# More table-sum steps in high and low parts, and VectorE constants read by pointer, in the product-key stage of an audio tower

## The reference

```python
k = einsum('bnhk,bnhkd->bnhd', kv_scores, keys_table[ind])
v = einsum('bnhk,bnhkd->bnhd', kv_scores, values_table[ind])
attn = softmax(where(causal, einsum('bihd,bjhd->bhij', q, k), neg))
out = einsum('bhij,bjhd->bhid', attn, v)
```

## Time and profile before

| what | value |
|---|---|
| median of 3 runs | 2059.56 us (2059.18 to 2062.91) |
| the profiled execution, its own time | 2059.58 us |
| its span | 2057.8 us, so 1.8 us lie around it |
| granted TensorE clock, mean | 0.97; 1.00 in every stretch of 200 us from 500 us on |
| busy, share of the span | PE 94%, PEld 73%, DVE 84%, ACT 72%, POOL 61% |
| third stage | from about 275 us to the end |

### The profile page before, as it was taken

How to read it: one execution, slowest core, us unless ns; L and a number is a source line. 1 busy time by engine, 2 the same in 40 slices (tenths; PEclk the granted TensorE clock), 3 DMA queues, 4 the chain that set the end, 5 groups by cost and what they waited for, 6 DMA issues and landing times.

```text
span 2057.8 us, 43660 instructions
## 1 busy us (share of the span) xinstructions
PE 1942.7 (94%) x11396; PEld 1509.4 (73%) x11396; DVE 1724.5 (84%) x5163; ACT 1486.5 (72%) x3091; POOL 1265.2 (61%) x1300
## 2 busy tenths in 40 slices
PE   5996649999999999999999999999999999999997
PEld 3983437777777777777777777777777777777776
DVE  3562659999989989999999899999999899999996
ACT  3564236787777777777777777787778777777775
POOL 2440106667766666677677667666766666676664
PEclk9998768999999999999999999999999999999998
DMA  3000030000100020001000100001000100010001
GB/s 97 1 0 0 1 103 16 18 14 19 62 20 19 19 62 18 18 17 59 18 19 19 58 23 19 19 19 60 17 17 16 60 19 19 19 61 19 19 17 27
DMA packets 118154, 58.06 MB, mean 28 GB/s; under 512 B 109712, under 2 KB 116048, under 8 KB 116813
## 3 DMA queue, kind: packets, MB, share of 16 engines
q1 hardware_dynamic: 115298, 56.75, 10.2%
q10 hardware_dynamic: 2795, 0.70, 0.2%
HBM read 24.55 MB, written 0.70 MB: 12 GB/s over the span
## 4 chain that ended last, share of the span: by engine, by line
PE 79%; issue 2%; DVE 1%; SPq 1%; DMA 1%; POOL 1%; ACT 1%; DVEq 0%; ACTq 0%; POOLq 0%
PE ps L988 27%; PE ps L996 15%; PE ps L979 15%; PE ps L1000 7%; PE ps L1038 4%; PE ps L1056 3%; PE ps L973 2%; PE ps L1048 2%; PE ps L1023 2%; SPq L931 1%; DMA k_X<-k_spl 1%; PE ps L1010 1%; PE ps L1016 1%; POOL k_W_low L1322 0%; PE ps L1039 0%
## 5 line engine op out<-in xcount | busy, mean ns | idle before, releaser
L1322 POOL TENSOR_TENSOR k_W_low<-k_W,k_W_high 128x688 fp32r<-128x688 f32 x513 | 852.3, 1661 | 379.0 <-ACT k_W_high L1164 379.0
L1159 ACT ACTIVATE k_W<-ps 128x688 f32<-128x688 f32 x1029 | 765.6, 744 | 391.3 <-PE ps L979 373.9
L1441 DVE SCALAR_TENSOR_TENSOR k_W<-ps,k_W 128x688 f32<-128x688 f32 x1028 | 888.8, 865 | 164.0 <-ACT k_W L1159 144.4
L988 PE MATMUL ps<-k_W,k_tab 128*128 128x344 f32 x2048 | 676.9, 453 | 0.0
L979 PE MATMUL ps<-k_X,k_sel 128*128 128x344 f16 x2058 | 473.8, 312 | 26.7 <-DMA k_X<-k_spl 13.5
L988 PEld LDWEIGHTS ps<-k_W,k_tab 128*128 128x128 f32 x2048 | 367.2, 190 | 127.2 <-issue 0.6
L1164 ACT ACTIVATE k_W_high<-k_W 128x688 fp32r<-128x688 f32 x513 | 395.4, 771 | 0.0
L996 PE MATMUL ps<-k_W_high,k_tab_high 128*128 128x344 f32 x1024 | 385.7, 379 | 0.0
L979 PEld LDWEIGHTS ps<-k_X,k_sel 128*128 128x128 f16 x2058 | 170.9, 99 | 216.0 <-issue 82.6
L996 PE MATMUL ps<-k_W_high,k_tab_low 128*128 128x344 f32 x1024 | 324.9, 320 | 0.0
L1000 PE MATMUL ps<-k_W_low,k_tab_high 128*128 128x344 f32 x1024 | 244.4, 320 | 0.0
(11 more groups left out here) (228 smaller groups left out, 2567.3 us busy)
## 6 DMA issues: line engine op xcount, KB each, us to landing
k_tab<-in_tables SPq DMA_DIRECT2D x9, 2048.0 KB, 7.2
k_X<-k_spl SPq DMA_TRANSPOSE x390, 2.4
k_xs<-x2T SPq DMA_DIRECT2D x33, 172.0 KB, 2.1
k_qT<-k_qs SPq DMA_DIRECT2D x33, 86.0 KB, 2.0
cst<-in_consts SPq DMA_DIRECT2D x1, 1024.0 KB, 19.0
wts<-in_weights SPq DMA_DIRECT2D x1, 896.0 KB, 13.0
cst<-in_consts SPq DMA_DIRECT2D x1, 874.5 KB, 16.7
xr<-in_xrows SPq DMA_DIRECT2D x1, 750.0 KB
```

Source lines behind the costliest of these rows:

```text
L988: mm = mm_(sums, tab[:, slot, at + k, :], W[:, d % RING, k, :], start=(d == 0 and k == 0), stop=(d == NDC - 1 and k == 1))
L1159: A(W[:, d % RING, :, :], ps[:, 2 * (d % 2):2 * (d % 2) + 2, 0:LOUT], ACT.Exp).then_inc(e_done, 1)
L1322: G.tensor_tensor(W_low[:, q % SPLIT_RING, :, :], W[:, d % RING, :, :], W_high[:, q % SPLIT_RING, :, :].bitcast(F32), ALU.subtract).then_i ...
L1441: V.scalar_tensor_tensor(W[:, d % RING, :, :], ps[:, 2 * (d % 2):2 * (d % 2) + 2, 0:LOUT], 0.0, W[:, d % RING, :, :], ALU.is_ge, ALU.mult) ...
```

## The change

Steps 1, 2, 3, 5, 7, 9, 10, 11, 13 and 15 are split: steps 2 and 10 join the eight. Of each window of 8 table chunks 6 are now held in parts (3 of 4 steps; tab_high and tab_low grow from 32 to 48 chunks a side, and an eighth of the table from two chunks to three). Ten steps are no multiple of the ring's 4, so `part_slot` also counts by the item's parity. P and PT of the attention now lie in parts of the constants' tile that are free by then. The attention output moves on PE from behind step 13 to behind step 14, and DVE's `add_output` from step 14 to step 15. The constants of `clamp_scores` and `floors` lie in a tile `bounds` of 128x4, filled once by four memsets at the start, and the four operations read them as 128x1 operands. Left out below: the handing of `cst` into the function, and the further argument `par` of `weights_high` and `weights_low` where they are called.

```diff
@@ -778,18 +778,18 @@
         NDC = NCH // 2
         WINDOW = (0, 2, 3, 1)
         STEPS = 6 + 6 + 6 + 1 + 3 + 3 + 2 + 3
-        SPLIT = (1, 3)
-        SPLITS = [d for d in range(NDC) if d % 4 in SPLIT]
+        SPLIT = (1, 2, 3)
+        SPLITS = [1, 2, 3, 5, 7, 9, 10, 11, 13, 15]
         NSPLIT = len(SPLITS)
-        NPART = 2 * NSPLIT // 8
-        FIRST_ROW = (2, 6)
+        NPART = len(SPLIT)
+        FIRST_ROW = (2, 5)
         RING, SPLIT_RING = 8, 4
         LEAD = 5
         MID0, MID1 = 6, 7
 
         tab = sb("tab", [128, 2, NCH, 128])
-        tab_high = sb("tab_high", [128, 2, 2 * NSPLIT, 128], F32R)
-        tab_low = sb("tab_low", [128, 2, 2 * NSPLIT, 128], F32R)
+        tab_high = sb("tab_high", [128, 2, 8 * NPART, 128], F32R)
+        tab_low = sb("tab_low", [128, 2, 8 * NPART, 128], F32R)
         wqh = sb("wqh", [128, 2, 128])
         wos = sb("wos", [128, H, D])
         pkw_sb = sb("pkw_sb", [DKEY, H, 128])
@@ -809,6 +809,8 @@
         small = sb("small", [128, 5, NT])
         MX, AM, FLOOR, DT, EDT = range(5)
         off = sb("off", [128, NT])
+        bounds = sb("bounds", [128, 4])
+        UPPER, LOWER, MARGIN, DEPTH = (bounds[:, k:k + 1] for k in range(4))
         ecs = sb("ecs", [128, NT, NCAND])
         zs = sb("zs", [128, NT])
         gain = sb("gain", [128, 2, NT])
@@ -826,11 +828,11 @@
         vw = sb("vw", [128, NT, D])
         qT = sb("qT", [128, 2, LOUT])
         qs = sb("qs", [64, LOUT])
-        P = sb("P", [128, NT, LOUT])
+        P = cst[:, CONST["cos"][0]:CONST["decay"][1]].rearrange("p (t s) -> p t s", t=NT)
         nmax = sb("nmax", [128, NT])
         zz = sb("zz", [128, NT])
         rz = sb("rz", [128, NT])
-        PT = sb("PT", [128, NT, LOUT])
+        PT = cst[:, CONST["sel"][0]:CONST["sel"][0] + NT * LOUT].rearrange("p (t s) -> p t s", t=NT)
 
         s_tab, tab_high_ready, tab_low_ready = [sem("s_tab0"), sem("s_tab1")], sem("tab_high_ready"), sem("tab_low_ready")
         high_done, low_done = sem("high_done"), sem("low_done")
@@ -864,6 +866,10 @@
 
             return SPLITS.index(d)
 
+        def part_slot(d, par):
+
+            return (split_at(d) + NSPLIT * par) % SPLIT_RING
+
         def split_before(d, back):
 
             k = split_at(d) - back
@@ -993,11 +999,11 @@
                         pe.wait_ge(high_done, i * NSPLIT + (q + 1))
                         for k in range(2):
                             for t in (tab_high, tab_low):
-                                mm_(sums, t[:, slot, at + k, :], W_high[:, q % SPLIT_RING, k, :],
+                                mm_(sums, t[:, slot, at + k, :], W_high[:, part_slot(d, par), k, :],
                                     start=(d == 0 and k == 0 and t is tab_high), stop=False)
                         pe.wait_ge(low_done, i * NSPLIT + (q + 1))
                         for k in range(2):
-                            mm = mm_(sums, tab_high[:, slot, at + k, :], W_low[:, q % SPLIT_RING, k, :], start=False,
+                            mm = mm_(sums, tab_high[:, slot, at + k, :], W_low[:, part_slot(d, par), k, :], start=False,
                                      stop=(d == NDC - 1 and k == 1))
                     mm.then_inc(main_done, 1)
 
@@ -1118,7 +1124,7 @@
                                 attention_scores(i, nj, g)
                             if d == 11:
                                 turn_probabilities(i, nj)
-                            if d == 13:
+                            if d == 14:
                                 attention_output(i)
 
                 rounds(pe, Body)
@@ -1158,10 +1164,10 @@
                     act.wait_ge(log_mm, i * NDC + (d + 1))
                     A(W[:, d % RING, :, :], ps[:, 2 * (d % 2):2 * (d % 2) + 2, 0:LOUT], ACT.Exp).then_inc(e_done, 1)
 
-                def weights_high(i, d):
+                def weights_high(i, d, par):
                     act.wait_ge(main_done, i * NDC + (split_before(d, SPLIT_RING) + 1 + ahead(main_done)))
                     act.wait_ge(w_done, i * NDC + (d + 1))
-                    A(W_high[:, split_at(d) % SPLIT_RING, :, :], W[:, d % RING, :, :], ACT.Copy).then_inc(high_done, 1)
+                    A(W_high[:, part_slot(d, par), :, :], W[:, d % RING, :, :], ACT.Copy).then_inc(high_done, 1)
 
                 def table_high(slot, loads, pair, half):
 
...
@@ -1316,10 +1322,10 @@
                     G.tensor_tensor(spl[:, :, :, 1, :], aS[:, :, :, :],
                                     spl[:, :, :, 0, :], ALU.subtract).then_inc(low_step, 1)
 
-                def weights_low(i, d):
+                def weights_low(i, d, par):
                     q = split_at(d)
                     pool.wait_ge(high_done, i * NSPLIT + (q + 1))
-                    G.tensor_tensor(W_low[:, q % SPLIT_RING, :, :], W[:, d % RING, :, :], W_high[:, q % SPLIT_RING, :, :].bitcast(F32),
+                    G.tensor_tensor(W_low[:, part_slot(d, par), :, :], W[:, d % RING, :, :], W_high[:, part_slot(d, par), :, :].bitcast(F32),
                                     ALU.subtract).then_inc(low_done, 1)
 
                 def table_low(slot, head, pair, half):
...
@@ -1412,8 +1418,8 @@
                         V.match_replace(rc[:, t, :], fin[:, t, 0:8], cand[:, t, :], NEG).then_inc(top_step, 1)
 
                 def floors(n):
-                    V.tensor_scalar(small[:, AM, :], small[:, AM, :], -DELTA, None, ALU.mult).then_inc(top_step, 1)
-                    V.tensor_scalar(small[:, FLOOR, :], fin[:, :, 0], -80.0, None, ALU.add).then_inc(top_step, 1)
+                    V.tensor_scalar(small[:, AM, :], small[:, AM, :], MARGIN, None, ALU.mult).then_inc(top_step, 1)
+                    V.tensor_scalar(small[:, FLOOR, :], fin[:, :, 0], DEPTH, None, ALU.add).then_inc(top_step, 1)
 
                 def threshold(n):
 
@@ -1425,9 +1431,9 @@
 
                 def clamp_scores(n):
                     dve.wait_ge(a_ready, n * 2 + 2)
-                    V.tensor_scalar(aS[:, :, 4, :], aS[:, :, 0, :], -NEG, FAR, ALU.min, ALU.max).then_inc(clamped, 1)
+                    V.tensor_scalar(aS[:, :, 4, :], aS[:, :, 0, :], UPPER, LOWER, ALU.min, ALU.max).then_inc(clamped, 1)
                     dve.wait_ge(clamped, n * 2 + 1)
-                    V.tensor_scalar(aS[:, :, 0:4, :], aS[:, :, 0:4, :], -NEG, FAR, ALU.min, ALU.max).then_inc(clamped, 1)
+                    V.tensor_scalar(aS[:, :, 0:4, :], aS[:, :, 0:4, :], UPPER, LOWER, ALU.min, ALU.max).then_inc(clamped, 1)
 
                 def softmax_sum(n):
                     dve.wait_ge(z_step, n * 2 + 2)
@@ -1491,10 +1497,12 @@
                 V.memset(top[:, 2, :, :], 0.0).then_inc(zeroed, 1)
                 V.memset(gain[:, :, :], 0.0).then_inc(zeroed, 1)
                 V.memset(zz[:, :], 1.0).then_inc(zeroed, 1)
+                for bound, value in ((UPPER, -NEG), (LOWER, FAR), (MARGIN, -DELTA), (DEPTH, -80.0)):
+                    V.memset(bound, value).then_inc(zeroed, 1)
                 cast(sel[:, :, :, :].rearrange("p w c m -> p (w c m)"), "sel")
                 cast(eyeb[:, :], "eye")
                 cast(causb[:, :], "causal")
-                dve.wait_ge(zeroed, 10)
+                dve.wait_ge(zeroed, 14)
                 def chosen(n):
                     dve.wait_ge(mx_ready, n + 1)
                     for t in range(NT):
@@ -1572,6 +1580,7 @@
                                 halves_max(i + 2, True)
                             if d == 14:
                                 largest_score(i + 2)
+                            if d == 15:
                                 add_output(i, pair * 2 if par else ((pair + 3) % 4) * 2 + 1)
 
                 rounds(dve, Body)
```

More of the change, by code:

```diff
@@ L91, in audio_tower @@
             retention(nc, ps, hT, x2T, epst, const, weight)
-        product_key_attention(nc, ps, hT, x2T, const, pkw, wq, wo, tables, out)
+        product_key_attention(nc, ps, hT, x2T, cst, const, pkw, wq, wo, tables, out)
 def token_mixer(nc, ps, hT, const, weight, bias, epst, cst, wts, bia, consts, xrows, xcols, weights, biases):
@@ L753, in _, with product_key_attention @@
                 layer_norm(1)
-def product_key_attention(nc, ps, hT, x2T, const, pkw, wq, wo, tables, out):
+def product_key_attention(nc, ps, hT, x2T, cst, const, pkw, wq, wo, tables, out):
     with ExitStack() as ctx:
@@ L1218, in _ @@
                     if d in SPLITS:
-                        weights_high(0, d)
+                        weights_high(0, d, 0)
                 class Body:
@@ L1235, in item @@
                                 if d + LEAD - 2 < NDC:
-                                    weights_high(i, d + LEAD - 2)
+                                    weights_high(i, d + LEAD - 2, par)
                                 else:
-                                    weights_high(i + 1, d + LEAD - 2 - NDC)
+                                    weights_high(i + 1, d + LEAD - 2 - NDC, 1 - par)
                             if d == 2:
@@ L1341, in _ @@
                     if d in SPLITS:
```

(6 more changed lines are left out.)

## The result

The changed kernel takes 2124.88 us, the median of 4 runs (2116.72 to 2131.53), against 2059.98 us before: a ratio of 1.030 (95% interval 1.027 to 1.033). It is slower, as forecast, but by 65 us where 13.7 were worked out. The profiled execution took 2131.53 us (span 2129.7).

What follows compares the result with a forecast made beforehand. PE was taken as the bound, with one wait per item caused by POOL through DVE. -26.9 + 35.8 + 3.3 + 1.5 = +13.7 us on 2059.6 gave 2073 us; range 2018 to 2090, the likeliest case's own 2062 to 2090.

Steps and rivals of the forecast that it cites:

- The bound and the way: Third stage: PE is the bound, with one wait per item (0.18 us before) that POOL causes by way of DVE.
- the walk: Steps 14 to 3, timed from the earlier trace: POOL's W_low ends 0.36 us later, PE starts step 3 at 1021.74.
- Two shorter steps, -26.9 us: PE's steps 2 and 10, split, each take 0.21 us less in 64 items, if all else is in time.
- The gap of 0.74 us, +35.8 us: Ahead of PE's step 3: the wait grows from 0.18 to 0.74 us in each of 64 items, if L1415 stays held.
- 1.5: At the start: four memsets and wider table parts on ACT and DVE add 1.5 us.
- The pointer, +3.3 us: Second operation of floors (L1416): reading its constant by pointer costs 0.05 us in 64 items; bounds 0 and 6.6 us.
- The pointer does not take the operation out of POOL's way: First operation of floors (L1415): still held until POOL's W_low ends, median rising from 879 ns to about 1.25 us.
- rival 1: Floors (L1415): the pointer frees it from POOL and the gap goes; 2023 us, up to 2036; chance 0.32.
- The move costs nothing: Attention output behind step 14 and `add_output` in step 15 only move, at no cost.
- The margin of 0.08 us behind step 10: PE after split step 10: 0.08 of 0.29 us margin is left, counted as 0; bounds 0 and 0.2 us per item.
- The range: Whole kernel: 2018 to 2090 us, to hold 8 in 10; the likeliest case's own range 2062 to 2090.
- The sign: Whole kernel: slower than before by more than 4 us, chance 0.53; faster 0.37, within 4 us 0.10.

Runs made afterwards that it cites:

- kernel 4: The changed kernel with floors as six operations on 128x1 elements, and floors and clamp constants as immediates: 2031.92 us.
- run 7: The changed kernel with all four constants as immediates, and POOL's centre_second waiting until both operations of floors are done: 2078.40 us.
- runs 1 and 2: The changed kernel with only the two constants of floors as immediates, 2105.39 us, and with all four constants as immediates, 2103.27 us.
- run 3: The kernel before with only the four constants read by pointer, with the tile `bounds` and its four memsets: 2086.45 us.
- run 9: The changed kernel with floors as 128x1 operations and immediates, the attention output back behind step 13 and DVE's part in step 14: 2025.94 us.
- run 2: The changed kernel with all four constants as immediates, so the split steps and the moved output alone: 2103.27 us.

## Why the prediction was right and wrong

By its own steps:

- **The bound and the way** (PE waits for the W of step 6, late by a hold under POOL's W_low). Right, and each time of the walk up to the end of that hold was met within 0.03 us in the trace after. What stands behind it was missed by 0.42: the W of step 6 starts at 1006.22, where the walk, moved by the same 15.02 us, has 1005.80, and PE's step 3 at 1007.14 for 1006.72.
- **Two shorter steps, -26.9 us.** Right: step 2's and 10's work is 1.25 us each, and kernel 4 gets the gain.
- **The gap of 0.74 us, +35.8 us.** Right as far as it went, for the first operation: 0.79 us in run 7, in which this hold alone is left. That run is 2078.40 - 2062.42 = 16 us above before, where -26.9 + 35.8 + 1.5 makes +10.4.
- **The pointer, +3.3 us.** This is the step that failed. I wrote that only the second operation "has its extra on the way from the lock to W", at 0.05 us, and so took this way as free once the W_low has ended. It is not free: the second operation (L1422) is held behind POOL's next one, L1281, for 0.40 us in each ordinary item, 0.40 x 64 = 26 us. Half of it is the pointer's: with immediates every other item is free of it (runs 1 and 2), so in the changed kernel the pointer costs 0.40 x 32 = 13 us, and in the kernel before, where no item was held, it costs 25 (run 3). The other half, also 13 us, comes with the new split steps alone. My upper bound, 6.6 us, was made of latencies, not of what POOL starts next, though this operation stood there in the earlier trace rows (L1275 in the kernel before).
- **Left out: the holds over several operations of POOL.** I took a hold to last for one operation, as in the rows of before, where the maximum was 891 ns. In four items it lasts 4 us, and with the lower clock behind it this is about 16 us.
- **The pointer does not take the operation out of POOL's way.** Right, and with rival 1 out by run 3. What set L1422 of before apart was the single element, not the second pointer: kernel 4 is rival 1's case by another way, at 2031.92 where 2023 to 2036 had been worked out.
- **The move costs nothing.** 6 us off (run 9). The margin of 0.08 us behind step 10 held in the ordinary items: step 11 takes 1.81 to 1.84 us where it took 1.80, step 12 is as before.
- **The range** ended at 2090. Its upper end was made of bounds on terms that I had; the hold of the second operation and the long holds were missing. The sign was right for the reason given, as the first hold alone makes the change a loss (run 7), but two thirds of the size came from what the sum did not have.

The runs put the whole together. By the medians: before 2060; the steps in their place with all holds (run 2) +42; the pointers +22 (2124.88 - 2103.27), of which up to 8 us (2124.88 - 2116.72) may be the clock in the second stage. By the items: the first hold with the two shorter steps 0.26 x 64 = 17 us (run 7), the second hold 26, the long holds 16, together 59 where 57.5 was measured.

The Trainium skill's conditions for the two-port mode (page "VectorE: DVE Perf Modes", section "What auto-detection actually checks") ask that the outermost dimensions larger than one be both even or equal, and nothing of the constant. Run 3 agrees, as operations of 128x3 are held with a pointer too. An operation of 128x1 has no such dimension; run 4 shows that it is never held. The Trainium skill's sentence on the page "SBUF — State Buffer", section "Who interferes with whom", that whoever issues first gets the pair for the whole instruction, agrees with the ordinary item, where L1421 ends 0.02 to 0.03 us behind POOL's W_low. It does not cover the hold of 4.06 us over several operations.

## What to carry to other kernels

Where two engines exclude each other, do not take the short operation behind a held one as free: ask what the other engine starts next, and price the chance of waiting for all of that. The distance of the recorded starts does not answer this (it was about 20 ns in items won and in items lost), so a change of form or of place needs a run. Any added work on the other engine right ahead of it lengthens the hold. Keep tiny operations on a critical chain in a form that was never held (here three 128x1 operations for one of 128x3), before adding work to the engine that holds them. And a queue that stops for a moment can be worth more than one that never idles: one wait on POOL brought 25 us.

## What was not expected of the hardware

- A 128x3 `tensor_scalar` of 0.16 us by itself (0.22 with a pointer) took 4.06 us while POOL ran four operations back to back: DVE does not always get its turn at the end of an operation.
- The same operation on one element per partition (139 to 149 ns in run 4) is never held, though 380 of the 390 lie within a POOL operation.
- Behind an idle time of 3.51 us PE's granted clock was 0.50 (814 to 817 us), so that the wait cost 1.5 us more than itself.
- The granted clock of the untouched second stage differs from execution to execution (0.60 or 0.72 from 250 to 300 us) and moves the start of the third stage by 15 us.
